# Graph attention and a routed feed-forward layer on one core: the turning of expert rows is issued one block earlier, with four row buffers instead of three

## The reference, cut to what matters

```
x = x + gat(layernorm(x), src, dst)     # 2500 nodes, 80000 edges, 256 features, 4 heads
x = x + ffn(layernorm(x))               # 8 experts, each token goes to its best 2

def ffn(x):                             # D = 256, H = 512, DOUT = 256
    xn = layernorm(x) * gamma + beta
    logits = xn @ Wr + br
    w_full = softmax over the 2 largest logits, 0 elsewhere
    for e in range(8):
        h   = gelu(xn @ W1[e] + b1[e])
        y  += (h @ W2[e] + b2[e]) * w_full[:, e]
```

## Time and profile before

| what | value |
|---|---|
| three timed executions | median 1513.36 us (1510.36 to 1515.03) |
| profiled execution, its own time | 1508.79 us |
| its span in the profile | 1507.0 us |
| PE / PEld busy over the span | 52% / 41% |
| DVE / POOL / ACT busy over the span | 50% / 53% / 8% |

### The profile page before, as it was taken

The page is one execution under the profiler, slowest core; times in us unless marked ns, Lnnn a source line. Parts: engine busy times, 40 slices in busy tenths (PEclk is TensorE's granted clock), DMA queues, the critical chain, the costliest instruction groups (busy, mean ns, idle before and its releaser), DMA issues.

```text
span 1507.0 us, 10576 instructions
## 1 busy us (share of the span) xinstructions
PE 788.1 (52%) x2990; PEld 617.4 (41%) x2990; DVE 757.1 (50%) x1578; ACT 120.4 (8%) x289; POOL 792.2 (53%) x843
## 2 busy tenths in 40 slices
PE   0610204454654555644555644545567288888881
PEld 0500203333443343433433433334447266766661
DVE  5510206555576555676555765555878822222215
ACT  3400000000000000000000000000002221111110
POOL 6357763666666666766666766666200034434431
PEclk9865556767787767877768777778776589999985
DMA  8254332333333333333333333333270111111116
GB/s 305 84 74 115 108 85 57 93 91 97 103 95 92 93 97 91 103 94 90 94 97 93 101 94 91 94 98 99 85 265 12 64 44 56 53 52 54 54 48 218
DMA packets 76401, 144.34 MB, mean 96 GB/s; under 512 B 19951, under 2 KB 46749, under 8 KB 76221
## 3 DMA queue, kind: packets, MB, share of 16 engines
q0 software_dynamic: 39856, 110.32, 26.1%
q1 hardware_dynamic: 33909, 30.82, 6.9%
q10 hardware_dynamic: 2584, 2.56, 0.5%
HBM read 126.85 MB, written 17.43 MB: 96 GB/s over the span
## 4 chain that ended last, share of the span: by engine, by line
DVE 33%; another core or an unknown queue 22%; issue 18%; PE 12%; DMA 6%; POOL 5%; DVEq 3%; ACT 2%; SPq 0%; POOLq 0%
DVE acc L1080 8%; DVE shared L1153 6%; DMA ring<-z_tab,ring 4%; DVE ring L1151 4%; PE psum L640 3%; PE psum L736 3%; POOL ys_tab L523 3%; PE psum L750 2%; POOL ring L514 1%; DVEq L1080 1%; PE psum L724 1%; PE psum L569 1%; DVE shared L1387 1%; DVE ring L1152 1%
## 5 line engine op out<-in xcount | busy, mean ns | idle before, releaser
L503 POOL DMA_INDIRECT ring<-h_tab,srcP x664 | 629.1, 947 | 328.9 <-issue 190.1
L640 PE MATMUL psum<-ring,shared 128*128 128x260 f32 x1328 | 417.7, 483 | 236.4 <-DVE acc L1080 156.3
L640 PEld LDWEIGHTS psum<-ring,shared 128*128 128x128 f32 x1328 | 320.2, 247 | 325.1 <-DVE shared L1153 175.2
L1151 DVE TENSOR_TENSOR ring<-ring,psum 128x2048 f32<-128x2048 f32 x83 | 189.5, 2283 | 9.1 <-PE psum L631 2.4
L1080 DVE TENSOR_TENSOR acc<-acc,psum 128x260 f32 x332 | 140.1, 422 | 95.4 <-remote 44.1
L1091 DVE TENSOR_TENSOR_SCAN edY<-RS_all,psum 128x128 f32<-128x128 f32 x21 | 8.8, 421 | 300.8 <-remote 268.5
L523 POOL DMA_INDIRECT ys_tab<-shared,ring x54 | 56.2, 1040 | 150.2 <-DVE shared L1387 142.0
L514 POOL DMA_INDIRECT ring<-z_tab,ring x54 | 52.6, 973 | 151.3 <-DVEq L1367 135.2
L736 PE MATMUL psum<-ring 128*128 128x256 f32 x432 | 114.1, 423 | 29.4 <-DVE ring L1379 29.4
L614 PE MATMUL psum<-ident,Fw 128*1 128x128 f32 x21 | 7.8, 373 | 216.6 <-DVEq L1096 215.0
L1379 DVE TENSOR_SCALAR ring<-psum,tail_consts 128x256 f32<-128x256 f32 x54 | 26.9, 539 | 185.8 <-PE psum L724 182.6
(11 more groups left out here) (290 smaller groups left out, 656.2 us busy)
## 6 DMA issues: line engine op xcount, KB each, us to landing
ring<-h_tab,srcP POOLq DMA_INDIRECT x664
ring<-in_L_ffn_W SPq DMA_DIRECT2D x16, 512.0 KB, 9.7
h_tab<-ring SPq DMA_DIRECT2D x10, 260.0 KB
ring<-in_x SPq DMA_DIRECT2D x1, 2432.0 KB
z_tab<-ring SPq DMA_DIRECT2D x2, 1024.0 KB, 4.4
ring<-ys_tab SPq DMA_DIRECT2D x4, 512.0 KB, 8.8
ring<-ys_tab ACTq DMA_DIRECT2D x4, 512.0 KB, 9.7
out<-acc SPq DMA_DIRECT2D x4, 512.0 KB
```

The source lines that it names most:

```text
L503: pool.indirect_dma_start(out=ring[:, t % RING, :], out_offset=None, in_=h_tab, in_offset=bass.IndirectOffsetOnAxis(ap=srcP[:, t:t + 1], a ...
L640: last = pe.matmul(bank[g][:, 0:MW], dst_oh[:, n % OHB, 2 * g + r, :], ring[:, t % RING, :], start=(r == 0), stop=(r == 1))
L1151: v.tensor_tensor(msg, msg, ex.unsqueeze(3).broadcast_to([P, BT, H, FO]), ALU.mult)
```

## The change

T(j+2) is issued between L1(j+1) and L2(j), where T(j+1) stood ahead of L1(j+1). T(1) moves ahead of L1(0). `xs_in` gets a fourth buffer, and since POOL's loop is written in terms of `XB`, its order becomes: fetches 0, 1, 2, 3; then for each j: fetch j+3 (left out for j = 0), put j. TensorE's order becomes T(0), T(1), L1(0), and then for each j: L1(j+1), T(j+2), L2(j). No instruction is added or removed.

```
-        XB = 3
+        XB = 4
...
             slots_T(0)
+            slots_T(1)
             layer_1(0)
             for j in range(NBLK):
                 if j + 1 < NBLK:
-                    slots_T(j + 1)
                     layer_1(j + 1)
+                if j + 2 < NBLK:
+                    slots_T(j + 2)
                 layer_2(j)
```

## The result

The changed kernel takes 1447.99 us in the median (1445.53 to 1450.26, four runs) against 1513.28 us (1510.36 to 1515.03): a ratio of 0.957 (95% interval 0.9548 to 0.9592), 65 us less. The prediction was 1449.5 us, with a range of 1443 to 1462. The profiled execution took 1445.53 us, 63.3 less than that of before.

The account below looks back on a forecast made before the run. TensorE, near full, was held by bare DVE copies, a one-block DMA ring and a low clock; 26 x 1.33 + 18.4 + 11.25 less 1.0 is 63.2, checking 63.8 gained: 1449.5 us against 1513.4, range 1443 to 1462.

Parts of the forecast that it names:

- The bare copies: TensorE waits 1.33 us a block for the two DVE copies between T and L1; L2 laid over them hides all.
- the ring: T, L2, bias, put, fetch, next T: 12.3 us over two blocks against TensorE's 14.7; 18.4 us of DMA waits go.
- the clock: Six slow first layers on TensorE, each following a T that waited for DMA; their 11.25 us excess goes with the waits.
- The slower rival: The ring closes over one block, 12.3 us a block against 9.82: 62 us more, 1575 us; 2 in 100.
- The sum: L1(26) starts 62.1 us earlier and is itself 1.7 faster: 63.8 us gained, 1449.5 us against the median.
- T(1) ahead of L1(0): At the start T(1) must wait for the second fetch, so L1(0) starts 1.0 us later.
- The transition from T to L2: New neighbours on TensorE: taken at nothing, though 0.24 us a block, 6 us in all, was kept for the range.
- the slack: Time to spare in the two-block ring, 2.4 us, with POOL needing about 5.0 us of a block's 7.37, 68%.
- The rival of a binding ring: Slower fetches and POOL issues stretch the two-block ring to about 15.7 us: 12 us more, 1461 us; 9 in 100.

Follow-up runs that it names:

- the run without DMA waits: Kernel before with four row buffers instead of three and the old TensorE order: 1326.67 us against 1354.86 (0.9797).
- a gather: One more indirect DMA between put j and the fetch: 1454.72 us (16-byte rows, changed kernel) or 1454.11 (1 KB rows, three buffers), against 1505.18 before.
- the fills: Changed order, three buffers, fetch j+3 issued by hand, plus three POOL memsets of 512 columns between put j and fetch: 1446.08 us against 1505.18 before.
- the gather ahead of it: Changed order, three buffers, fetch j+3 first, then one more 1 KB-row gather, then put j: 1292.55 us against 1355.59 before (0.9534).

## Why the prediction was right

**The bare copies.** 1.33 us a block were to go, all of them. The row is gone, and the run with four buffers alone shows it by itself: with the ring and the clock out of the way, 8.70 us stay, against 7.35 with the new order. From that run's stage to the changed kernel's are 230.9 - 195.5 = 35.4 us, and the wait for the copies was 36.0. Right.

**The ring.** It was to span two blocks, 12.3 us against 14.7. In the changed kernel T(2)'s load at 1219.95 to bias is 4.42 us (4.54 put down), put and fetch follow at the distances of the earlier trace rows, and the DMA waits behind the start, 18.4 us net, are all gone. What the ring has to spare can be read from the fetch of block 4: 5.07 us from its second issue to T(4), less the 2.75 of a usual landing, leaves 2.3, where 2.4 was put down. That both halves of the diff are needed was said, and is shown: the order alone is 107 us slower. That "without the fourth buffer fetch j+3 would stand behind put j" holds only as the loop is written; the buffer can be spared if the fetch is moved by hand.

**The slower rival** was priced at 12.3 us a block from rows at the upper clock; measured, it is 14.5, since the wait that it brings slows the second layer inside the same ring: from T to bias are 6.2 us (1178.64 to 1184.84) instead of 4.54. As 62 us it was mis-sized, against 107 measured; the expectation of that run (62 to 130) had the clock in it and held.

**The clock.** 11.25 us were counted as gained. PEclk is 1.00 from 1216 us on, the second block, and no layer behind is slow. Both the run without DMA waits, in which no slow layer is left, and the one with waits put in say that it was the waits. The first of them also says that the 1.33 us for the copies alone doesn't bring the low clock, in 26 blocks out of 26. Why only six of the 19 DMA waits did is not known, and the forecast didn't need it.

**The sum.** The stage got shorter by 260.5 - 195.5 = 65.0 us, where 63.8 were put down. A block is 7.346 us instead of 7.37, which is 0.6 of it; L1(0) and L1(1) loaded in 8.44 us together instead of 5.76 + 3.34, which is 0.7. T(1) ahead of L1(0) cost what was said: first load of T(0) to that of L1(0) is 3.23 us (1208.25 to 1211.48) against 2.21 before, 1.0 more. The graph layer, untouched, was 1.7 us longer in this execution, hence 63.3 over all. The transition from T to L2, taken at nothing, costs nothing (0.54 us from T's first load to L2's).

**What was too bright** is a number on which the forecast did not hang: the slack. 2.4 us in the ring and 68% of POOL seemed to leave room for 1.29 us more. But 2.4 holds for a landing of 2.75 us. With the slowest landing, 4.00, the prediction's own ring is 13.5 us of 14.7, and 1.2 is left, less than a gather's 1.3 or the fills' 1.7. The fills show just that: T waits only where a landing takes 3.7 us or more, and the whole price is 6 us. With a gather, 14 us on the chips of 1505 us, late releases of DVE and ACT come on top, for which the earlier trace rows have no row. The rival of a binding ring, 9 in 100, was priced at 12 us by a slower ring.

Open: whether one more indirect DMA costs because it stands between put and fetch, or only on the chips that show late releases; neither the gather behind put j on a chip of 1355 us nor the gather ahead of it on one of 1505 was measured. Open too: what releases DVE and ACT late.

## What to carry to other kernels

When an engine waits a little for one thing and a little for another in the same loop, write down for each wait the ring that it closes and how many iterations the ring spans. The longest ring by its span sets the pace, and hiding a stall in another can lengthen it; here the same reordering is worth minus 65 us or plus 107 us by where one fetch stands in POOL's queue. Count the clock that comes back with the waits, and price a slower case at the lower clock too. Take a ring's slack with the slowest landing in the rows, not with the usual one: here that is 1.2 us instead of 2.4.

## What the runs showed of the hardware that was not expected

Chips differ: the same kernel takes 1355 or 1505 to 1514 us, most of it in a layer in which POOL issues 664 indirect DMAs one behind the other, 0.3 us apart. In the traces of the latter POOL itself has 78 to 93 us there of waits without a known releaser, 19 to 29 of them, up to 7.8 us each. With POOL waiting some 2.3 us a block for the bias, as in the changed kernel, the expert stage shows none of them on either; with 1.3 us of it filled by another gather the DVE copies are released late in two to seven of 27 blocks, on the slower chips; with 1.7 us of it filled by fills, in none.

A wait of 5 us on TensorE costs about 7.5: four of them, 20.4 us, made the stage 30.3 us longer (226.0 against 195.7), with the next transposes at 1.1 instead of 0.6 us and the next 16 matmuls at 5.2 to 5.9 instead of 3.6. The Trainium skill ("TensorE: Matmul & The Clock Gate", Part 1), which has activity release a low default clock, fits all four; no run here shows why it is so.
